# A four-layer decoder: folding coefficients loaded earlier, row sums copied by ScalarE, the last down product in f32r parts

## What is computed

```python
# layer 0, feed-forward: x @ W_exp, ten butterfly stages over 1024 features, gelu,
# ten butterfly stages back, @ W_con
def butterfly(y, weights, dim):
    for stage in range(weights.shape[0]):
        s = 2 ** stage
        a, b = the two halves of each block of 2 * s features
        na  = w[..., 0, 0] * a + w[..., 0, 1] * b
        nb2 = w[..., 1, 0] * a + w[..., 1, 1] * b
# layers 1 and 2, mixer: softmax attention, 16 heads of 16 (layer 1 causal, layer 2 full)
# layer 3, feed-forward: top 4 of 16 experts by a softmax router, each expert
# gelu(x @ w1 + b1) @ w2 + b2 with 512 hidden features, weighted and summed
```

## Time and profile before

| | |
|---|---|
| median of 3 runs | 2581.3 us (2570.56 to 2587.81) |
| the profiled execution's own time | 2578.14 us |
| its span | 2576.4 us |
| mean granted TensorE clock | 0.914 |
| TensorE busy | 2279.8 us (88%), VectorE 1404.3 (55%), ScalarE 1129.9 (44%), GpSimd 644.5 (25%) |

### The profile page before, as it was taken

One profiled execution on the slowest core, in us unless ns is written; L12 is line 12 of the kernel. 1 busy time (PEld: TensorE's weight loads), 2 busy tenths in 40 slices (PEclk: granted clock), 3 DMA queues, 4 the chain that ended last, 5 costly groups with the idle time before them and its releaser, 6 DMA issues. The chain is left out here.

```text
span 2576.4 us, 41981 instructions
## 1 busy us (share of the span) xinstructions
PE 2279.8 (88%) x15258; PEld 1519.6 (59%) x15258; DVE 1404.3 (55%) x3517; ACT 1129.9 (44%) x1927; POOL 644.5 (25%) x868
## 2 busy tenths in 40 slices
PE   1789999998899999949999998799998898699996
PEld 1678754444345799924444444467665545589995
DVE  5625377885464221268999955666566555411114
ACT  6543345655342111135777774522443334234444
POOL 6010232321211033231111002100356311245551
PEclk8789978988998999967999999789999898799998
DMA  6100132220113199832131101031111210599996
GB/s 231 34 1 1 34 55 44 46 46 18 30 35 119 58 332 332 304 105 47 26 51 26 26 7 46 2 115 38 31 27 19 57 18 26 209 297 350 356 342 234
DMA packets 86512, 268.89 MB, mean 104 GB/s; under 512 B 25354, under 2 KB 43906, under 8 KB 70300
## 3 DMA queue, kind: packets, MB, share of 16 engines
q1 hardware_dynamic: 70628, 233.10, 29.6%
q0 software_dynamic: 15680, 33.12, 4.1%
HBM read 207.36 MB, written 23.94 MB: 90 GB/s over the span
## 5 line engine op out<-in xcount | busy, mean ns | idle before, releaser
L1667 ACT ACTIVATE prob<-st_ps 128x1024 f32<-128x1024 f32 x448 | 412.8, 933 | 215.3 <-PE st_ps L1534 213.9
L1687 DVE TENSOR_REDUCE cmax<-ring 128x1 f32<-128x512 f32 x640 | 401.4, 683 | 40.2 <-PE ring L1542 37.7
L3133 PE MATMUL A<-xbT,w 128*128 128x128 f32 x2512 | 301.8, 276 | 1.1 <-DMA w<-L1f_W_dram 0.5
L3133 PEld LDWEIGHTS A<-xbT,w 128*128 128x128 f32 x2512 | 291.6, 193 | 1.9 <-DMA w<-L1f_W_dram 0.8
L1581 PE MATMUL acc<-prob,v 128*32 128x256 f32 (+2 forms) x3200 | 265.5, 405 | 13.6 <-DVE byq L1725 12.6
L3377 DVE COPY yb<-C 128x256 f32<-128x256 f32 x118 | 50.1, 424 | 285.3 <-PE C L3141 282.4
L3050 POOL DMA_INDIRECT y_rows_dram<-yb,dst x118 | 116.3, 986 | 326.1 <-DVE yb L3377 322.9
L3141 PE MATMUL C<-w,hid 128*128 128x256 f32 x632 | 149.3, 379 | 0.0
L1534 PE MATMUL st_ps<-qst,kst 64*128 64x512 f32 (+3 forms) x560 | 135.6, 482 | 7.3 <-DMA qst<-parts 3.2
L3037 POOL DMA_INDIRECT xb<-x_rows_dram,src x118 | 115.0, 975 | 99.7 <-DVE src L3347 64.4
L1683 DVE CUSTOM_DVE_ANT_0 masked<-ring,causal_wide 128x512 bf16<-128x512 f32 (+3 forms) x256 | 112.5, 487 | 44.2 <-PE ring L1542 43.3
(11 more groups left out here) (478 smaller groups left out, 4471.0 us busy)
## 6 DMA issues: line engine op xcount, KB each, us to landing
w<-L3f_W_dram SPq DMA_DIRECT2D x79, 1026.0 KB
w<-L1f_W_dram SPq DMA_DIRECT2D x39, 1536.0 KB
room<-y_rows_dram SPq DMA_DIRECT2D x8, 1024.0 KB, 10.1
kst<-parts SPq DMA_DIRECT2D x120, 64.0 KB, 2.4
qst<-parts SPq DMA_DIRECT2D x120, 64.0 KB, 2.4
gate<-L2f_gates_dram SPq DMA_DIRECT2D x5, 1536.0 KB, 7.4
first<-parts SPq DMA_DIRECT2D x96, 64.0 KB, 2.4
qT<-dense SPq DMA_DIRECT2D x84, 64.0 KB, 2.4
```

The costliest lines, as they stand in the source:

```text
L1667: act.activation(prob[:, step % PROBS, 2 * p:2 * p + 2, 0:n], st_ps[:, p, :, 0:n], ACT.Exp, scale=scale)\
L1687: dve.tensor_reduce(cmax[:, a, t:t + 1, k0 // CH], spot(key)[:, 0:k1 - k0], AX.X, ALU.max)\
L3133: mm = pe.matmul(A[:, j % 2 * 2 + a, f * TB:(f + 1) * TB], up_w(w[:, j % WB], a, k, f), xbT[:, j % 2, k, :], start=(k == 0), stop=(k == KT ...
```

## The change

In folding, `coef_d` becomes a ring of six, and SyncE's order changes: coefficients 2 to 4 of the down side go ahead of W_con, all five of its second chain ahead of the wait for `down_kept`, up side coefficients 6 and 7 too; the pad masks go behind that wait, and x and ctxT go last. In stacked attention the transposed maxima are freed and copied by ScalarE instead of VectorE, and `turned` stands between a step's third and fourth maximum instead of behind the fourth. In the last routed stage w2 and the hidden values are each split into an f32r high and low part, the high by a copy and the low by a subtraction (w2 by ScalarE and VectorE, the hidden values by VectorE), and `drop` is three f32r products for each float32 one. Some tiles of that stage move into `env.wide` and `env.xT`. Layer 1's routed stage keeps its float32 `drop`.

The diff, with the semaphores' names and unchanged lines cut:

```diff
@@ -522,7 +522,8 @@
...
     coef_u = env.w3[:, :, :, :].rearrange("p i o (f j) -> p i o f j", j=SUB)
-    coef_d = sbuf(nc, st, "coef_d", [P, 2, 2, NB8, SUB])
+    RU, RD = 3, 6
+    coef_d = sbuf(nc, st, "coef_d", [P, RD, 2, NB8, SUB])
@@ -533,11 +534,11 @@
...
     B = psum(nc, st, "B", [P, NB8, D])
...
     u_ready = (s.coef_u0, s.coef_u1, s.coef_u2)
-    d_ready = (s.coef_d0, s.coef_d1)
+    d_ready = (s.coef_d0, s.coef_d1, s.coef_d2, s.coef_d3, s.coef_d4, s.coef_d5)
@@ -549,44 +550,48 @@
...
             for i in range(first, first + n):
-                if i >= 3:
-                    sp.wait_ge(s.u_step, steps_done(i - 3))
-                sp.dma_start(coef_u[:, i % 3], dram["coef"][i]).then_inc(u_ready[i % 3], 16)
+                if i >= RU:
+                    sp.wait_ge(s.u_step, steps_done(i - RU))
+                sp.dma_start(coef_u[:, i % RU], dram["coef"][i]).then_inc(u_ready[i % RU], 16)
...
             for i in range(first, first + n):
-                if i >= 2:
-                    sp.wait_ge(s.d_step, steps_done(i - 2))
-                sp.dma_start(coef_d[:, i % 2], dram["coef"][2 * STEPS + i]).then_inc(d_ready[i % 2], 16)
+                if i >= RD:
+                    sp.wait_ge(s.d_step, steps_done(i - RD))
+                sp.dma_start(coef_d[:, i % RD], dram["coef"][2 * STEPS + i]).then_inc(d_ready[i % RD], 16)
...
         down_coefs(1, 1)
-        up_coefs(1, 2)
+        up_coefs(1, 1)
+        down_coefs(2, 2)
+        up_coefs(2, 1)
+        down_coefs(4, 1)
         sp.dma_start(down_rows[:, :, :], dram["W_con"]).then_inc(s.down_loaded, 16)
+        up_coefs(3, 1)
...
         begin.load_x(sp, 3)
-        for i in range(3):
-            down_coefs(2 + i, 1)
-            up_coefs(3 + i, 1)
+        up_coefs(4, 1)
...
         sp.dma_start(ups[:, 0, :], dram["up_bias"]).then_inc(s.up_bias_loaded, 16)
-        begin.load_pads(sp)
-        down_coefs(STEPS, 2)
+        up_coefs(5, 1)
+        down_coefs(5, 5)
+        up_coefs(6, 2)
...
         sp.dma_start(dram["fold_down"].rearrange("(p r) d -> p r d", p=P), down_rows[:, :, :]).then_inc(s.down_stored, 16)
-        up_coefs(6, 4)
+        up_coefs(8, 1)
+        begin.load_pads(sp)
+        sp.wait_ge(s.down_stored, 16)
+        sp.dma_start(down_rows[:, :, :], dram["fold_down"].rearrange("(f n) d -> n f d", n=P)).then_inc(s.down_back, 16)
+        sp.wait_ge(s.up_kept, 2)
+        sp.dma_start(dram["fold_up"].rearrange("(f n) d -> n f d", n=P), up_rows[:, :, :]).then_inc(s.up_stored, 16)
+        up_coefs(9, 1)
+        sp.wait_ge(s.up_stored, 16)
+        sp.dma_start(up_rows[:, :, :], dram["fold_up"].rearrange("(p r) d -> p r d", p=P)).then_inc(s.up_back, 16)
...
         sp.dma_start(env.ctxT[:, :, :], dram["ctxT"].rearrange("(k p) t -> p k t", p=P)).then_inc(s.x_loaded, 16)
-        sp.wait_ge(s.down_stored, 16)
-        sp.dma_start(down_rows[:, :, :], dram["fold_down"].rearrange("(f n) d -> n f d", n=P)).then_inc(s.down_back, 16)
-        down_coefs(STEPS + 2, STEPS - 2)
-        sp.wait_ge(s.up_kept, 2)
-        sp.dma_start(dram["fold_up"].rearrange("(f n) d -> n f d", n=P), up_rows[:, :, :]).then_inc(s.up_stored, 16)
-        sp.wait_ge(s.up_stored, 16)
-        sp.dma_start(up_rows[:, :, :], dram["fold_up"].rearrange("(p r) d -> p r d", p=P)).then_inc(s.up_back, 16)
@@ -612,16 +617,16 @@
...
             stride = 2 ** (STEPS - 1 - t if down else t)
-            now = coef_d[:, i % 2] if down else coef_u[:, i % 3]
+            now = coef_d[:, i % RD] if down else coef_u[:, i % RU]
...
             if down:
-                eng.wait_ge(d_ready[i % 2], 16 * (i // 2 + 1))
+                eng.wait_ge(d_ready[i % RD], 16 * (i // RD + 1))
             else:
-                eng.wait_ge(u_ready[i % 3], 16 * (i // 3 + 1))
+                eng.wait_ge(u_ready[i % RU], 16 * (i // RU + 1))
@@ -1268,7 +1273,7 @@
...
         for n in turns_due(c):
-            enter(("turn", n), 1)
+            enter(("turn", n), 0)
@@ -1548,7 +1553,7 @@
...
                         pe.transpose(spot(key)[0:HU * TH, 0:P], negc[:, n % 2].rearrange("p a t -> p (a t)"), env.ident[:, :])\
-                          .then_inc(s.dve_filled, 1)
+                          .then_inc(s.act_filled, 1)
@@ -1644,6 +1649,12 @@
...
                 def extras(c):
+                    for n in turns_due(c):
+                        key = ("turn", n)
+                        act.wait_ge(s.act_filled, filled(key))
+                        if n >= 2:
+                            act.wait_ge(c_loaded[n % 2], 32 * (n // 2))
+                        act.activation(crow[:, n % 2, :], spot(key)[0:HU * TH, 0:P], ACT.Copy).then_inc(s.act_freed, 1)
@@ -1707,12 +1718,6 @@
...
                         negate(c)
-                    for n in turns_due(c):
-                        key = ("turn", n)
-                        dve.wait_ge(s.dve_filled, filled(key))
-                        if n >= 2:
-                            dve.wait_ge(c_loaded[n % 2], 32 * (n // 2))
-                        dve.tensor_copy(crow[:, n % 2, :], spot(key)[0:HU * TH, 0:P]).then_inc(s.dve_freed, 1)
@@ -1748,9 +1753,11 @@
...
                     if c is not None:
-                        pieces(c, (0, 1))
+                        pieces(c, (0,))
...
                         turned(step - LAG)
+                    if c is not None:
+                        pieces(c, (1,))
@@ -2882,14 +2889,14 @@
...
         b2 = sbuf(nc, st, "b2", [E, D])
-        sc = sbuf(nc, st, "sc", [P, NT, E])
+        sc = env.wide[:, 4 * KT * P:4 * KT * P + NT * E].rearrange("p (t e) -> p t e", t=NT) if biased else sbuf(nc, st, "sc", [P, NT, E])
...
         idf = sbuf(nc, st, "idf", [P, NT, K])
-        eq = sbuf(nc, st, "eq", [P, NT, K, E])
+        eq = env.wide[:, 0:NT * K * E].rearrange("p (t k e) -> p t k e", t=NT, k=K) if biased else sbuf(nc, st, "eq", [P, NT, K, E])
@@ -2920,14 +2927,19 @@
...
         w = early.w if early else sbuf(nc, st, "w", [P, WB, ROW])
-        xb = sbuf(nc, st, "xb", [P, XB, D])
+        flat_xT = env.xT[:, :, :].rearrange("p k t -> p (k t)")
+        xb = flat_xT[:, 0:XB * D].rearrange("p (x d) -> p x d", x=XB) if biased else sbuf(nc, st, "xb", [P, XB, D])
...
         else:
-            act, hid = None, sbuf(nc, st, "hid", [P, 2, NF, TB])
-        yb = sbuf(nc, st, "yb", [P, 4, D])
+            act, hid = None, flat_xT[:, (XB + 4) * D:(XB + 4) * D + 2 * NF * TB].rearrange("p (x f n) -> p x f n", x=2, f=NF)
+            hid_hi = sbuf(nc, st, "hid_hi", [P, 2, NF, TB], F32R)
+            hid_lo = sbuf(nc, st, "hid_lo", [P, 2, NF, TB], F32R)
+            down_hi = sbuf(nc, st, "down_hi", [P, 2, NF * D], F32R)
+            down_lo = sbuf(nc, st, "down_lo", [P, 2, NF * D], F32R)
+        yb = flat_xT[:, XB * D:(XB + 4) * D].rearrange("p (x d) -> p x d", x=4) if biased else sbuf(nc, st, "yb", [P, 4, D])
@@ -2977,6 +2989,9 @@
...
             return src_w[:, at:at + D]
+
+        def down_rows(j):
+            return w[:, j % WB, NW * KT * F:NWE]
@@ -3134,7 +3149,21 @@
...
+            def drop_in_parts(j):
+                pe.wait_ge(s.down_low, j + 1)
+                pe.wait_ge(s.hid_low, j + 1)
+                to = room_c(("drop", j))
+                for f in range(NF):
+                    cols = slice(f * D, (f + 1) * D)
+                    pe.matmul(to, hid_hi[:, j % 2, f, :], down_hi[:, j % 2, cols], start=(f == 0), stop=False)
+                    pe.matmul(to, hid_hi[:, j % 2, f, :], down_lo[:, j % 2, cols], start=False, stop=False)
+                    mm = pe.matmul(to, hid_lo[:, j % 2, f, :], down_hi[:, j % 2, cols], start=False, stop=(f == NF - 1))
+                mm.then_inc(s.down_done, 1)
+
             def drop(j):
+                if biased:
+                    drop_in_parts(j)
+                    return
@@ -3211,6 +3240,14 @@
...
+            def raise_down(j):
+                act_e.wait_ge(w_ready[j % WB], 16 * (j // WB + 1))
+                if j >= 2:
+                    act_e.wait_ge(s.down_done, j - 1)
+                act_e.activation(down_hi[:, j % 2, :], down_rows(j), ACT.Copy).then_inc(s.down_high, 1)
+
+            if biased:
+                raise_down(0)
@@ -3224,11 +3261,13 @@
...
                     if j >= 2:
-                        act_e.wait_ge(s.down_done, j - 1)
+                        act_e.wait_ge(s.hid_low, j - 1)
...
                     a.then_inc(s.hid_ready, 1)
+                    if j + 1 < NBLK:
+                        raise_down(j + 1)
@@ -3376,7 +3415,25 @@
...
+            def lower_down(j):
+                dve.wait_ge(s.down_high, j + 1)
+                dve.tensor_tensor(down_lo[:, j % 2, :], down_rows(j), down_hi[:, j % 2, :].bitcast(F32), ALU.subtract).then_inc(s.down_low, 1)
+
+            def part_hid(j):
+                dve.wait_ge(s.hid_ready, j + 1)
+                if j >= 2:
+                    dve.wait_ge(s.down_done, j - 1)
+                dve.tensor_copy(hid_hi[:, j % 2], hid[:, j % 2]).then_inc(s.hid_high, 1)
```

(9 more changed lines are left out.)

4 lines of the change are left out of this document (2 added, 2 removed).

## The result

| | before | after |
|---|---|---|
| median | 2579.2 us (7 runs, 2570.6 to 2587.8) | 2556.4 us (7 runs, 2554.7 to 2561.0) |
| profiled execution, its span | 2578.1, 2576.4 us | 2561.0, 2559.3 us |
| mean granted clock | 0.914 | 0.917 |

The ratio is 0.9908, 95% interval 0.9890 to 0.9927: 23 us less, where 29 were forecast. The profiled execution of after is the slowest of its seven; between the two profiled ones the difference is 17. In what follows "before" and "after" are these two kernels.

The account below looks back on a forecast made before the run. Folding was taken as bound by waits, the second attention by VectorE, the last stage by busy TensorE with transfers barely keeping up. Folding -15, attentions -6 and last stage -8 us took 2578.1 to 2549, range 2531 to 2568.

Parts of the forecast that it names:

- R1: Rival: transfers already at their limit, last-stage blocks stay at 3.73 us, last stage +4, total 2561; chance 0.22.
- R2: Rival: folding gains only its second idle, 9 us, and the attentions nothing; total 2561; chance 0.1.
- (a): Folding: `coef_d` 2 to 4 issued before W_con, so the first down product starts about 6 us earlier.
- (b): Folding: chain 3's five coefficients load before the `down_kept` wait, so it runs through and ScalarE's second idle, 9 us, goes.
- (c): Folding's later copies: L684's product no longer queues behind L678 (gain up to 2) or runs slower (loss 1); taken as 0.
- (d), (e): Stacked attentions: `crow` copies moved to ScalarE, `turned` ahead of the last maximum; -6 us together, bounds -12 and +4.
- (f): Last routed stage: down product as twelve f32r products takes 1.40 us instead of 1.73, gain 0.33 us a block.
- (h): Last stage, first 17 blocks: a loop through `hold` and `lower_down` keeps 4.5 us a block; no gain, bounds -6 and +5.
- (i): Last stage, blocks 18 to 75: TensorE alone would give -19 us, the transfer bound -10; taken as -12.
- R4: Rival: more than forecast, transfers follow TensorE at 3.45 us a block and L684 comes earlier; total 2538; chance 0.15.
- (j): Last four blocks: ScalarE also makes `diag`, 5.0 us a block; last `hold` 21.2 us after block 75's L3133, +4 us.
- R3: Rival: VectorE and GpSimd hold each other up in the last stage, 4.8 us a block, total 2619; chance 0.08.

Follow-up runs that it names:

- the masks ahead: Kernel after with the pad masks' four transfers issued right behind the upper bias, not behind the wait for `down_kept`; gain over before 31.5 us (26.1 to 36.9).
- a lower_down of 0.69 us: Kernel after with `lower_down` reading one SBUF operand instead of two (low part left out); gain over before 31.5 us (26.8 to 36.1).
- half of the loads: Kernel after, but from block 6 of the last routed stage only up weights are loaded; gain over before 29.7 us (25.8 to 33.6).
- the last stage's part alone: Kernel before with only the last routed stage's part of the change; median 2573.0 us against 2581.2, gain 9.3 us (4.9 to 13.4).

## Why the prediction was right, and where not

Forecast 2549 (range 2531 to 2568), measured 2556.4. That is just past the upper edge of the forecast's own case (2541 to 2556), and nearer to the 2561 of R1 and R2 than to 2549; the sum had started from the profiled execution, and after's profiled execution took 2561.0, 17 us less and not 29. It is also a gain of under 1%, to which the prediction gave 0.34 against 0.58 for more. So the total doesn't tell the forecast from R1 and R2. The stages do: the blocks didn't stay at 3.73 (R1), and folding's first idle went (R2). Of the signs that it named, some came (the wait for `coef_d`, the first blocks at 4.5 us, ScalarE full in the last four blocks) and some didn't (L672 before 50 us, where it was 53.95; L720 ending at 81 to 85, where it was 87.0; the second attention shorter by 4 to 8; the plain blocks at 3.5 to 3.6). And one sign that it had named for being wrong did come, in small: ScalarE waits 1 us in folding for the first up product, which isn't VectorE's chain.

- **(a) Chain 2 earlier, 6 us.** Right in mechanism and size: the first down product started at 21.83 instead of 28.00.
- **(b) Chain 3 runs through, 9 us.** Here the forecast failed: 5 us in after, 1.7 to 5 over the six profiles. The step was "landing at about 37 us" for the pad masks. They were issued at 35.9 to 37.6 (I had seen that they stand behind a step of GpSimd, and put the issue too early) and took 6.2 us more to land, at 43.86. They are four transfers of under 10 KB, and a coefficient, the down rows' reload and the upper store, 2.3 MB together, were issued within 3 us of them. I had charged the masks' new place on SyncE to nobody, though VectorE's chain stood right behind them. With the masks ahead, folding gave 16.3 us (16.4 and 13.0 in two more profiles), where the forecast had 15. That isn't the forecast's sum exactly: 2 of it are the term (c), taken as 0, and 0.7 goes to the new wait for the first up product, which the forecast didn't have.
- **(c) L684.** It still queued behind L678 in after (now L683, 59.41 to 63.14; L689 starts at 62.99), only for less long, and it ran no slower: the wait fell from 3.06 to 2.22, gain 0.8, taken 0. Where it doesn't queue, with the masks ahead, the wait is 0.94: the "up to 2" of the forecast.
- **(d), (e) Attentions, 6 us.** By time 7 (4 to 11), but by trace less: the second, for which I had said 4 to 8, gave 1.7, and the first nothing that shows. That the term came out is luck as far as the traces go. The failing step is "VectorE bounds it": with TensorE at 96.9 of 100 and 10.2 us of waits the two engines take turns, and an engine relieved by 4.3 us waits for the other.
- **(f) Twelve f32r products, 0.33 us a block.** 0.294: the pitch fell from 3.734 to 3.440. The unit price came from products of 48 to 64 rows and held for the whole array to within 0.003 us a product.
- **(g)** Hidden as said: ScalarE 46.7 and VectorE 50.9 of 65 us.
- **(h) First 17 blocks, 4.5 us.** 4.56. The loop was the right one: hold ahead of lower_down gives 4.20, and so does a lower_down of 0.69 us.
- **(i) Plain blocks, 12 us.** 10.3 (212.85 to 202.53 us for 57 blocks), but not by my reason. I had a floor of 3.56 from a busy share of 0.95. There was none: the engines carried 384 GB/s at the same 0.95. TensorE's pace gave 16.8 us and late lifts took 6.4 back, in after, 3.5 and 5.4 in the two other profiles of this stage. The chain of after has weights ahead of the late lifts of blocks 60 and 74; the one of block 59 is ScalarE's (last section). That 12 lay near 10.3 is two errors that cancel, a pace put too slow and late lifts put at nothing. R1 fell. The rule of the Trainium skill that the prediction set beside the earlier trace rows ("DMA: Bandwidth & Descriptors", section "Where 436 GB/s comes from", about 358 GB/s) doesn't agree with this total: it went past that figure, though the weights alone (1.05 MB in 3.44 us) are 305 of the 384. That section has the figure as half of what two cores share, and here one core ran. R4 was right on the pace (3.45) and wrong that nothing would be late.
- **(j) Last four blocks, 4 us.** 21.5 us from the lift of block 75 to the last hold, forecast 21.2, 17.0 before. Part of the match is chance: the lift of block 76 came 0.5 us late in after, and five other profiles with this tail have 20.0 to 20.8, so the cost is 3 to 4 us.
- **R2** fell with the first idle, which went too; its size for folding, 9 us, was the measured one, by the wrong idle.
- **R3.** Its first half is real: a GpSimd row transfer waits for the end of a running VectorE product of two SBUF operands (0.99 becomes 1.73 us). The Trainium skill ("SBUF — State Buffer", section "SBUF: two separate sides") says that a VectorE instruction with two SBUF inputs and a GpSimd one that reads SBUF can't run at once: whichever starts first keeps the other out for the whole instruction. (The section that the prediction names tells it of a copy.) These traces agree where VectorE was first. The second half of R3, that VectorE waits in turn, didn't show, against that sentence: with GpSimd 0.31 us ahead the product still took 1.23 us. GpSimd had 0.6 us a block to spare, so it cost nothing.

By terms: folding 15 foreseen, 9 measured; attentions 6 and 7; last stage 8 and 8 to 9. The difference is in folding, and the masks' late landing is the largest part of it.

## What to carry to other kernels

When an issue order is rewritten, list for each transfer that moves back who waits for it, however small it is: with four transfers of under 10 KB late folding gained 7.5 to 10.9 us, with them ahead 13.0 to 16.4. An engine queue must not let work that another queue waits for (hold) stand behind work that is needed a block later (lower_down). And where two engines are each over 95% busy, relieving one bought little here (1.7 us for 4.3 taken away); time the stage, not its counters.

## What the runs showed of the hardware

- The DMA busy share is no measure of room: 0.95 at 350 GB/s, 0.95 at 384, 0.77 at 230.
- A GpSimd row transfer waits for the end of a VectorE product with two SBUF operands that is already running (0.99 becomes 1.73 us), and not for one that starts 0.3 us after it. A third of a microsecond of phase decides it, and the phase differed between two kernels with the same code in these blocks, and within one execution (with half of the loads the gather took 0.97 us up to block 60 and 1.84 in all but one block after it).
- ScalarE stood still for no wait that the trace shows, perhaps for its own code. In the kernel with the masks ahead, and in after:
```profile
2422.99 0.37 ACT L3235 ACTIVATE xbT<-B 128x256 f32<-128x256 f32 x1
2426.44 1.14 ACT L3266 ACTIVATE xT<-A,w 128x128 f32<-128x128 f32 x4 [3.08 <-DMA first<-parts]
```
```profile
2431.66 1.14 ACT L3266 ACTIVATE xT<-A,w 128x128 f32<-128x128 f32 x4 [2.00 <-PE A L3148]
```
The releaser named in the first is of no use; nothing that this Gelu waits for was late. A packet of 16 KB on the instruction queue started at 2424.31 and took 0.95 us, and the Gelu ran 1.2 us behind it; the last stage's part alone has the same picture at 2439.87 and 2441.89. It is the Gelu of block 57 each time, in after too: there it ran 1.4 us behind its products, 0.6 us after such a packet had started (2431.07) and 0.4 before its end. Block 59, whose lift stands behind the drop of block 57, was late in these three and in none of the other six kernels with the new last stage. Those have a packet at the same block, but it starts 0.6 to 2.3 us after that block's first product, and 2.7 to 2.8 in the three. That it is code is an inference from these coincidences; no run took the code away.
- One stage, the first attention, has lengths of 269 to 286 us over fourteen profiles, with mean granted clocks of 0.908 to 0.920 over the whole program; differences of 5 us between two profiles are no finding.
